# Router logits from the first norm's rows and the attention's output operands, in a one-core decoder layer

## The reference

```
x1 = layernorm(x + retention(x))             # 16 heads of 16, decayed scores, group norm over a sequence
x2 = layernorm(x1 + att(x1, ctx) @ Wo.T + bo)
logits = x2 @ router_w.T                     # 8 experts
p = softmax(logits); the two largest, scaled to sum 1
y  = sum over the two experts of p_e * (gelu(x2 @ w_fc[e] + b_fc[e]) @ w_proj[e] + b_proj[e])
out = layernorm(x2 + y)                      # a layernorm has no weights: (v - mean) * rstd
```

## Time and profile before

| what | us |
|---|---|
| median of 3 runs | 994.58 (993.51 to 995.72) |
| profiled execution | 990.76 |
| its span | 988.7 |
| TensorE busy in the span | 924.2 (93%) |
| TensorE weight loads busy | 822.0 (83%) |
| VectorE busy | 664.0 (67%) |
| ScalarE busy | 605.2 (61%) |
| GpSimd busy | 385.0 (39%) |
| row_max of 128x512 on VectorE (L1267), mean of 128 | 0.682 |

### The profile page before, as it was taken

The page is one execution under the profiler, slowest core; times in us unless marked ns, Lnnn a source line. Parts: engine busy times, 40 slices in busy tenths (PEclk is TensorE's granted clock), DMA queues, the critical chain, the costliest instruction groups (busy, mean ns, idle before and its releaser), DMA issues.

```text
span 988.7 us, 29856 instructions
## 1 busy us (share of the span) xinstructions
PE 924.2 (93%) x10845; PEld 822.0 (83%) x10845; DVE 664.0 (67%) x1977; ACT 605.2 (61%) x1528; POOL 385.0 (39%) x639
## 2 busy tenths in 40 slices
PE   5899999999999999999888999999999999999950
PEld 4788888888888888888667899999999999999950
DVE  3577777777877877877734677575755775665536
ACT  4556656656556666666446567565755765665536
POOL 0324555555544656664523522222222323232223
PEclk9999999999999999999989999999999999999985
DMA  8111141112111111122112453523435343533228
GB/s 279 50 34 56 61 142 45 56 55 66 56 49 45 62 56 61 55 64 85 44 30 44 119 130 58 138 44 53 129 53 139 79 103 53 129 48 46 45 37 336
DMA packets 57362, 79.91 MB, mean 81 GB/s; under 512 B 5728, under 2 KB 46048, under 8 KB 57120
## 3 DMA queue, kind: packets, MB, share of 16 engines
q1 hardware_dynamic: 41504, 58.50, 18.5%
q0 software_dynamic: 13536, 18.16, 10.8%
q10 hardware_dynamic: 2208, 1.73, 0.6%
HBM read 52.10 MB, written 29.71 MB: 83 GB/s over the span
## 4 chain that ended last, share of the span: by engine, by line
PE 79%; ACT 6%; DVE 5%; issue 4%; DMA 2%; SPq 1%; POOL 1%; ACTq 0%; DVEq 0%; POOLq 0%
PE bank L820 16%; PE bank L834 11%; PE bank L511 11%; PE bank L836 5%; PE bank L647 4%; PE bank L673 4%; PE bank L718 3%; PE bank L573 3%; PE bank L626 3%; PE bank L694 3%; PE bank L598 3%; PE bank L593 2%; ACT h_f L1161 2%; PE bank L732 2%; ACT last_out L1237 1%
## 5 line engine op out<-in xcount | busy, mean ns | idle before, releaser
L820 PE MATMUL bank<-xs_hi,w_both 128*128 128x256 f32 x1152 | 241.6, 287 | 0.0
L1155 ACT ACTIVATE h_parts<-bank,bfc_s 128x256 fp32r<-128x256 f32 x288 | 140.0, 486 | 155.3 <-PE bank L820 150.6
L1714 POOL DMA_INDIRECT residual_sum<-y_w,meta_i x72 | 116.9, 1624 | 300.4 <-DVE y_w L1532 267.0
L1490 DVE TENSOR_TENSOR h_parts<-h_f,h_parts 128x256 fp32r<-128x256 f32 x288 | 121.5, 426 | 143.9 <-ACT h_f L1161 138.4
L834 PE MATMUL bank<-w_both,h_parts 128*128 128x512 f32 x544 | 200.0, 398 | 1.1 <-DVE h_parts L1490 1.1
L820 PEld LDWEIGHTS bank<-xs_hi,w_both 128*128 128x128 f32 x1152 | 191.0, 190 | 7.8 <-issue 1.7
L820 PE MATMUL bank<-xs_lo,w_both 128*128 128x256 f32 x576 | 162.7, 282 | 0.0
L836 PE MATMUL bank<-w_both,h_parts 128*128 128x256 f32 x544 | 153.0, 281 | 0.0
L1161 ACT ACTIVATE h_f<-bank,bfc_s 128x256 f32<-128x256 f32 x288 | 139.4, 484 | 3.9 <-DVE h_parts L1490 3.4
L834 PEld LDWEIGHTS bank<-w_both,h_parts 128*128 128x128 f32 x544 | 102.5, 188 | 19.9 <-DVE h_parts L1490 3.5
L820 PEld LDWEIGHTS bank<-xs_lo,w_both 128*128 128x128 f32 x576 | 109.4, 190 | 0.1
(11 more groups left out here) (184 smaller groups left out, 2139.7 us busy)
## 6 DMA issues: line engine op xcount, KB each, us to landing
rows<-sent_rows SPq DMA_DIRECT2D x37, 258.0 KB
xc_raw<-in_turned SPq DMA_DIRECT2D x32, 256.0 KB, 3.0
w_raw<-in_w_fc SPq DMA_DIRECT2D x8, 1024.0 KB
w_raw<-in_w_proj SPq DMA_DIRECT2D x8, 1024.0 KB
x_t<-in_x SPq DMA_DIRECT2D x32, 128.0 KB, 2.2
residual_sum<-x_row SPq DMA_DIRECT2D x32, 128.0 KB, 1.7
last_in<-residual_sum SPq DMA_DIRECT2D x7, 512.0 KB, 7.3
result<-last_out SPq DMA_DIRECT2D x7, 512.0 KB, 2.7
```

Of the source, the lines that this page charges most:

```text
L820: last = mm(ps_h(g, j), w[:, at:at + P], v[:, k, :], start=(n == 0), stop=(n == 3 * NCH - 1))
L1155: A(h_hi[j % 4][:, :], ps_h(g, j), ACT.Gelu_apprx_tanh, bias=bias)
L1490: V.tensor_tensor(h_lo[j % 4][:, :], h_f[j % 2][:, :], h_hi[j % 4][:, :].bitcast(f32), ALU.subtract).then_inc(s["h_split"], 1)
L1714: G.indirect_dma_start(total, bass.IndirectOffsetOnAxis(meta_i[:, half:half + 1], 0), y_w[:, half, :], None, compute_op=ALU.add)\
```

## The change

With P the attention rows before the output projection, the rows ahead of the second norm are v = x1 + bo + P Wo.T, and x2 = (v - mean) * rstd. The logits of x2 are rstd * (v R - mean * colsum(R)), with R the router's weights turned. The change computes v R as x1 R + bo R + P (Wo.T R):

- **Once**, at the end of step 1 (`fold`, `fold_bias`, `fold_out`): the product Wo.T R, 256 x 8, is put beside `wo_s` as columns 256 to 263; bo R and the column sums of R go to `lg_c`. For it a second, turned form of Wo is loaded into a part of `w_raw`, which stands idle then, and SyncE waits for the fold before it loads the first expert's weights there. `got_late` counts one load more.
- **Per sequence**: `qx` also multiplies x1T with `rt_s` into columns 256 to 263 of its bank; ScalarE copies them to one of three `lg_x1` in `qx_out`. `att_proj` has 264 columns where it had 256.
- `lg_out` on VectorE is three linked operations behind `ln2_stats`: mean times column sums plus bo R, plus `lg_x1`, plus the 8 columns of `ps_f`. It leaves out rstd, which `pick` multiplies into the difference of the two largest; their order is the same without it.
- `x2_turn`, `logits` and `x2_T_out` are gone. `rank`, which overwrites the columns in `ps_f`, waits for `lg_out` of the next sequence where it waited for the first operation of `ln2_stats`; `o_turn` waits for `put`.
- In VectorE's even step `put` stands behind `ln2_norm`. The same moves are made in the drain and the slots beside it.

```diff
 wq_s = ab("wq_s", [P, NCH, C])
-wo_s = ab("wo_s", [P, NCH, C])
+wo_s = ab("wo_s", [P, NCH, C + E])
...
 l2rstd = ab("l2rstd", [P, 1])
-x2T = ab("x2T", [P, NCH, T])
+bo_T = ab("bo_T", [P, NCH, T])
+lg_c = ab("lg_c", [P, 2, E])
+lg_mean = ab("lg_mean", [P, 2, E])
+lg_x1 = [ab(f"lg_x1_{i}", [P, E]) for i in range(3)]
...
+wo_turned = w_raw[:, 0:NCH * C].rearrange("p (m n) -> p m n", m=NCH)
+RAW = slice(C, C + E)
+
...
                 .then_inc(s["consts_expert"], 16)
+            sp.wait_ge(s["folded"], 2)
+            apart(sp)
             load_weights(0)
...
         if first(c, 1):
-            pe.wait_ge(s["got_late"], 64)
+            pe.wait_ge(s["got_late"], 80)
         for m in range(NCH):
             for k in range(NCH):
                 last = mm(ps_g[:, m * P:(m + 1) * P], wq_s[:, k, m * P:(m + 1) * P], x1T[:, k, :],
                           start=(k == 0), stop=(k == NCH - 1))
+        for k in range(NCH):
+            last = mm(bank_g[:, RAW], x1T[:, k, :], rt_s[:, k, :], start=(k == 0), stop=(k == NCH - 1))
         last.then_inc(s["qx"], 1)
...
         pe.wait_ge(s["o_out"], c.n + 1)
-        if not first(c, 1):
-            pe.wait_ge(s["lg_out"], c.n)
+        if first(c, 2):
+            pe.wait_ge(s["folded"], 2)
+        else:
+            pe.wait_ge(s["rank_read"], c.n - 1)
         for i in range(HPT):
...
+    def fold():
+        pe.wait_ge(s["got_late"], 80)
+        for k in range(NCH):
+            tr(ps_f[:, k * P:(k + 1) * P], bo_s[:, k * P:(k + 1) * P], ident)
+        for k in range(NCH):
+            at = slice(C + k * E, C + (k + 1) * E)
+            for m in range(NCH):
+                mm(ps_f[:, at], wo_turned[:, m, k * P:(k + 1) * P], rt_s[:, m, :],
+                   start=(m == 0), stop=(m == NCH - 1))
+        for m in range(NCH):
+            last = mm(ps_f[:, C + 2 * E:C + 3 * E], stat_w, rt_s[:, m, :],
+                      start=(m == 0), stop=(m == NCH - 1))
+        last.then_inc(s["fold"], 1)
+
+    def fold_bias():
+        pe.wait_ge(s["folded"], 1)
+        for m in range(NCH):
+            last = mm(ps_f[:, 0:E], bo_T[:, m, :], rt_s[:, m, :], start=(m == 0), stop=(m == NCH - 1))
+        last.then_inc(s["fold"], 1)
+
     def att_proj(c):
         pe.wait_ge(s["att_back_out"], c.n + 1)
         for k in range(NCH):
-            last = mm(ps_f[:, 0:C], attT[:, k, :], wo_s[:, k, :], start=(k == 0), stop=(k == NCH - 1))
+            last = mm(ps_f[:, 0:C + E], attT[:, k, :], wo_s[:, k, :], start=(k == 0), stop=(k == NCH - 1))
         last.then_inc(s["att_proj"], 1)
-    def x2_turn(c):
-        pe.wait_ge(s["x2_done"], c.n + 1)
-        if not first(c, 1):
+    def rank(c):
+        if c.n < B - 1:
+            pe.wait_ge(s["lg_out"], c.n + 2)
+        else:
             pe.wait_ge(s["rank_read"], c.n)
-        for k in range(NCH):
-            last = tr(ps_f[:, k * P:(k + 1) * P], x2_row[c.r][0][:, k * P:(k + 1) * P], ident)
-        last.then_inc(s["x2_T"], 1)
-
-    def logits(c):
-        pe.wait_ge(s["x2_T_out"], c.n + 1)
-        for k in range(NCH):
-            last = mm(ps_f[:, 0:E], x2T[:, k, :], rt_s[:, k, :], start=(k == 0), stop=(k == NCH - 1))
-        last.then_inc(s["logits"], 1)
-
-    def rank(c):
...
             run(y_back, At(k))
-            run(x2_turn, At(k - 3))
             run(att_values, At(k - 2))
-            run(logits, At(k - 3))
             run(prep_v, At(k + 1))
             run(o_turn, At(k - 2))
             run(max_turn, At(k - 1))
@@ -780,13 +800,14 @@
             run(gn_mean, At(k))
             run(y_back, At(k))
             run(max_scores, At(k - 1))
-            run(x2_turn, At(k - 3))
             run(att_values, At(k - 2))
-            run(logits, At(k - 3))
             run(prep_v, At(k + 1))
             if k < B - 1:
                 run(o_turn, At(k - 2))
                 run(max_turn, At(k - 1))
+        if k == 1:
+            fold()
...
             (bo_s[:, :], bo.partition_broadcast(P), "got_late"),
+            (wo_turned, wo_o.rearrange("(m p) n -> p m n", p=P), "got_late"),
             (rt_s[:, :, :], router_t.rearrange("(k p) n -> p k n", p=P), "got_late"))
...
         act.wait_ge(s["qx"], c.n + 1)
+        if not first(c, 3):
+            act.wait_ge(s["lg_out"], c.n - 2)
+            apart(act)
+        A(lg_x1[c.n % 3][:, :], bank_g[:, RAW], ACT.Copy)
...
-    def x2_T_out(c):
-        act.wait_ge(s["x2_T"], c.n + 1)
-        A(x2T[:, :, :].rearrange("p k t -> p (k t)"), ps_f[:, 0:C], ACT.Copy).then_inc(s["x2_T_out"], 1)
+    def fold_out():
+        act.wait_ge(s["fold"], 1)
+        A(bo_T[:, :, :].rearrange("p k t -> p (k t)"), ps_f[:, 0:C], ACT.Copy)
+        for k in range(NCH):
+            A(wo_s[:, k, C:C + E], ps_f[:, C + k * E:C + (k + 1) * E], ACT.Copy)
+        A(lg_c[:, 0, :], ps_f[:, C + 2 * E:C + 3 * E], ACT.Copy, scale=-float(T * C)).then_inc(s["folded"], 1)
+        act.wait_ge(s["fold"], 2)
+        A(lg_c[:, 1, :], ps_f[:, 0:E], ACT.Copy).then_inc(s["folded"], 1)
...
     def lg_out(c):
-        dve.wait_ge(s["logits"], c.n + 1)
-        V.tensor_copy(lg[:, :], ps_f[:, 0:E]).then_inc(s["lg_out"], 1)
+        if first(c, 1):
+            dve.wait_ge(s["folded"], 2)
+        V.scalar_tensor_tensor(out=lg_mean[:, 0, :], in0=lg_c[:, 0, :], scalar=l2mv[:, 0:1], in1=lg_c[:, 1, :],
+                               op0=ALU.mult, op1=ALU.add).then_inc(s["lg_shift"], 1)
+        dve.wait_ge(s["lg_shift"], 2 * c.n + 1)
+        dve.wait_ge(s["qx_out"], c.n + 1)
+        V.tensor_tensor(lg_mean[:, 1, :], lg_x1[c.n % 3][:, :], lg_mean[:, 0, :], ALU.add)                    .then_inc(s["lg_shift"], 1)
+        dve.wait_ge(s["lg_shift"], 2 * c.n + 2)
+        V.tensor_tensor(lg[:, :], ps_f[:, RAW], lg_mean[:, 1, :], ALU.add).then_inc(s["lg_out"], 1)
     def pick(c):
         dve.wait_ge(s["lg_out"], c.n + 1)
@@ -1352,7 +1379,9 @@
         ch.link(V.max(top[:, :], lg[:, :]), apart)
         if not first(c, 1):
             dve.wait_ge(s["share_chain"], SHARE * (c.n - 1) + 1)
-        V.tensor_tensor(gap[:, :], top[:, 1:2], top[:, 0:1], ALU.subtract).then_inc(s["gap_done"], 1)
+        dve.wait_ge(s["ln2_rstd"], c.n + 1)
+        V.scalar_tensor_tensor(out=gap[:, :], in0=top[:, 1:2], scalar=top[:, 0:1], in1=l2rstd[:, 0:1],
+                               op0=ALU.subtract, op1=ALU.mult).then_inc(s["gap_done"], 1)
         ch.link(V.max_index(top_i[:, :], top[:, :], lg[:, :]))
...
             run(ln2_stats, At(k - 3))
+            run(lg_out, At(k - 3))
+            run(ln2_norm, At(k - 3))
             run(put, At(k - 4))
-            run(ln2_norm, At(k - 3))
             run(gn_moments, At(k))
             for r in range(NT):
                 run(att_max, At(k - 1), r)
             run(max_twice, At(k - 1))
             run(gn_centre, At(k))
-            run(lg_out, At(k - 3))
             run(ln1_stats, At(k))
             run(att_norm, At(k - 2))
             run(ln1_sum, At(k))
```

More of the change, by code:

```diff
@@ L61, in link, with decoder_kernel @@
             then(self.eng)
-def decoder_kernel(nc, x, turned, kv_blocks, w_qkv, gn_scale, gn_shift, wq_t, wk_t, wv_t, wo_t, bo,
+def decoder_kernel(nc, x, turned, kv_blocks, w_qkv, gn_scale, gn_shift, wq_t, wk_t, wv_t, wo_t, wo_o, bo,
                    router_t, w_fc, b_fc, w_proj, b_proj, decay_c, small_c, bits_c, out):
@@ L277, in decoder_kernel @@
             rden_done att_norm att_back att_back_out att_proj
-            ln2_chain ln2_var ln2_rstd x2_done x2_again x2_T x2_T_out logits lg_out
+            ln2_chain ln2_var ln2_rstd x2_done x2_again fold bo_turned folded lg_shift lg_out
             top_chain gap_done picked ranked rank_read put_chain placed share_chain shared
@@ L382, in _ @@
             sp.dma_start(bits_f, bits_c).then_inc(s["got_mix"], 16)
-            sp.dma_start(wo_s[:, :, :], wo_t.rearrange("(k p) n -> p k n", p=P)).then_inc(s["got_late"], 16)
+            sp.dma_start(wo_s[:, :, 0:C], wo_t.rearrange("(k p) n -> p k n", p=P)).then_inc(s["got_late"], 16)
             load(At(2))
@@ L789, in step @@
                         run(max_turn, At(k - 1))
+                if k == 1:
+                    fold()
+                    fold_bias()
             def between():
@@ L874, in rank_out @@
                     rank(At(B - 2))
-                if j == 8:
-                    x2_turn(At(B - 1))
-                if j == 10:
-                    logits(At(B - 1))
             def rank_last(j):
@@ L898, in drain @@
                 rank(At(B - 4))
-                x2_turn(At(B - 3))
                 max_scores(At(B - 1))
-                logits(At(B - 3))
                 att_values(At(B - 2))
@@ L920, in drain @@
                 fc0(6)
-                x2_turn(At(B - 2))
                 proj0(5)
                 fc0(7)
-                logits(At(B - 2))
                 pe.wait_ge(s["max_split"], B)
@@ L1098, in step @@
                     run(y_out, At(k))
-                    run(x2_T_out, At(k - 3))
                     run(o_out, At(k - 2))
@@ L1130, in step @@
```

(16 more changed lines are left out.)

## The result

The changed kernel took 1000.52 us (median of 4 runs, 998.82 to 1001.32) against 995.02 for the kernel before (4 runs): ratio on record 1.007, 95% interval 1.0051 to 1.0089 (the two medians alone give 1.0055). Timed again beside more runs it took 1002.63 (6 runs) against 993.10 (17 runs): 1.0101, 1.0077 to 1.0125. So it is slower by 0.5 to 1.3%. The forecast was 1007, the added sum 12.3 us.

A forecast was written before the change was run, and what follows sets the result against it. TensorE bounds the steady stage, with VectorE close behind at four places. Pairs 8.1, load 0.7, fold 3.0, early raw product 0.5 and drain 0 sum to 12.3 us: 1003.1, plus 3.8 carried over, 1007 us; own range 1002 to 1012, overall 992 to 1013.

The forecast's parts named there:

- The pair: Two attention steps in the steady stage: 0.38 + 0.20 = 0.58 us longer, +8.1 us over 14 pairs.
- The raw product: Added TensorE product of x1T with the router weights, four passes behind L617: 0.45 us per sequence (0.45 to 0.54).
- third view: Weight loads set beside VectorE's timeline: four places stand close to VectorE, with 0.03 to 0.22 us of room.
- the gap operation: VectorE operation taking a third input at no extra price; if 0.1 more in even steps, +1.4 us over 14 pairs.
- The drain: Last stage: removed work against the raw product at the lower clock and the lg links; 0, between -2.7 and +2.4 us.
- The start: First steps: load +0.7, fold +3.0 and raw product in steps 0 to 2 +0.5 us.
- The load's 0.7: Turned output weights, 0.26 MB more in the queue that brings the padding at the start: +0.7 us (0 to 0.7).
- the fold's own 3.0: Fold at the end of step 1 delays step 2's scores by 3.1 us, some tenths absorbed: +3.0 us (1.5 to 4).
- rival 4: New idle time costs TensorE its clock, falling once behind the fold: 5 us, giving 1012 us; chance 0.04.
- Rival 1: TensorE alone is the bound and the new waits don't come: 992 us, or 987; chance 0.20.
- Rival 2: Half of the new waits is absorbed, rooms at L664 and L711 being larger than read: 1002 us; chance 0.12.
- Rival 3: The three lg links and the wait before rank reach the path in even steps: +7 us, 1014; chance 0.07.

The follow-up runs named there:

- delay: The kernel before with one spare 128x256 VectorE addition ahead of the row_max copy in odd steps; 998.80 us in a single run.
- raw_late: The changed kernel with the raw product, and ScalarE's copy of it, moved from qx to ahead of the max transpose; 993.64 us, 1.0013 to the kernel before.
- no_raw: The changed kernel without the raw product from the second sequence on; routing differs, so only pairs compare: 29.994 us a pair.
- pick_late: best0 with VectorE's choice of experts moved behind the retention masks (ret_p) in half of the steps; 999.02 us, 1.0061 to the kernel before.
- best0: The changed kernel with the edits of raw_late and fold_mid together; 993.14 us, 1.0004 to the kernel before.
- before_again: The kernel before, unchanged, run once more; 993.15 us.
- fold_mid: The changed kernel with the fold spread in step 2 and the turned weights loaded separately behind the padding; 999.53 us, 1.0055 to the kernel before.

## Why the prediction was right, and where its sizes were off

- **The mechanism stands.** The sum said that TensorE's shorter work would turn into a wait for the row_max copy, with the raw product paid in full behind it. The wait is there, 0.64 us on the weight load where 0.54 was forecast, each pair. TensorE's busy share is 97.6 (97 forecast). delay shows that the room was 0.08 us, raw_late that place and not length decides, no_raw that the removals without the raw product are worth 0.05 us a pair.
- **The pair: +0.58 forecast, +0.34 measured.** The raw product was mis-sized: 0.35 us, not 0.45, twice a pair, 0.20 in all. I took the time of four passes of 128 columns for four of 8. The remaining 0.04 is a balance of errors that nearly cancel:
  - At the attention scores the kernel before waited 0.25 us for ret_p (block 1.97), and the later scores of the changed kernel don't (1.72): a fifth place near VectorE that my third view missed, since no idle time names it. This took 0.25 off.
  - From the even scores to L711 a pair gained 0.22 (10.64 to 10.42) where 0.31 was forecast. The 0.09 is the lg copy, whose removal I counted in full. It had stood in the pause between the linked y_c and x_pre: from start to start they take 0.62 us with it and 0.61 without.

```profile
203.26 0.48 DVE L1290 SCALAR_TENSOR_TENSOR y_c<-bank,gm,gnw 128x256 f32<-128x256 f32 x1
203.66 0.16 DVE L1346 COPY lg<-bank 128x8 f32<-128x8 f32 x1
203.88 0.48 DVE L1298 SCALAR_TENSOR_TENSOR x_pre<-y_c,grstd,xb 128x256 f32<-128x256 f32 x1
```

```profile
181.68 0.48 DVE L1310 SCALAR_TENSOR_TENSOR y_c<-bank,gm,gnw 128x256 f32<-128x256 f32 x1
182.29 0.48 DVE L1318 SCALAR_TENSOR_TENSOR x_pre<-y_c,grstd,xb 128x256 f32<-128x256 f32 x1
```

  - The way from the odd L711's load to the scores' grew by 0.49 (205.71 to 209.47 before, 183.91 to 188.16 after); 0.38 of it is added work (0.35 + 0.03), 0.03 was forecast for L617, and 0.08 was not. There `pick` takes 0.14 longer ahead of x1 (MAX8 to x: 1.09 us, 0.95 before), as the prediction had feared of the gap operation with 0.1, and L617, now L625, waits for x1.
  - The last 0.04 lies between the odd scores and the next even ones; I didn't trace it.
- **The drain and what follows: 0 forecast, -1.4 measured** (with the end of the fourteenth pair in it), within what two runs of one kernel differ by (1.8 to 2.7 us). The bounds held; the value can't be judged.
- **The start: +4.2 forecast, +7.3 measured** (+5.6 to +7.3 over the four executions). The load's 0.7 is about right (0.8 at the padding's end). So is the fold's own 3.0 (2.91 and 2.75 on the chain, about 0.3 absorbed). The sum put the clock at nothing: rival 4, given 0.04 and 5 us, happened in part. Behind the fold the slower clock cost 1.5 and 1.7 us, and the first execution lost another 1.5 ahead of it, where the other fall stands (2.4 less the load's 0.8). That the fold at the end of step 1 brings the later fall is shown by five executions against eight; what in it does so is open. The 0.5 for the raw product in the first steps was not measured by itself. The step-2 scores started at 46.75, not near 45.
- **Rival 1** (TensorE alone is the bound) fell to the waits and to delay. Here the Trainium skill's rule (Perfetto Trace Analysis, Identifying the Most-Contended Engine) to optimize the engine of highest occupancy pointed the wrong way: TensorE at 150.00 of 150.00 gained next to nothing from less work (0.05 us a pair in no_raw), and by its weight loads it led as well (129.25 against VectorE's 116.34). Its warning that matmul busy time misleads held. **Rival 2** said +4 in the stage and 1002 us, which is about what came, and nearer to it than the forecast's +8.1 and 1007, but for another reason: it held that the rooms were larger than I read, and the rooms came out as read (0.08 us at L664 by delay, 0.22 at L711), with the wait at L674 longer than forecast, not shorter. **Rival 3** (links before rank) did not come: the rank product's loads wait 0.8 us for lg in ten pairs, four times in all. pick_late shows the place where it does come.
- **The total.** 12.3 us was forecast on a span of 988.7, 10.3 came. The 3.8 us carried over to the median of the runs should not have been: the kernel before repeated at 993.1 over 17 runs, and the changed kernel's profile lay at its own median. Two errors of more than 3 us, start (+3.1) and pairs (-3.3 over the same 14), had opposite signs; that the sum of 12.3 came within 2 us of the 10.3 is luck to that extent.

## What to carry over

When an engine reads as fully busy, set its waiting instructions beside the ends of their inputs: where that room is 0.1 us, two engines are the bound in turn, and an edit is worth only what the next wait behind it lets through. Put added work where the engine waits anyway, and expect the next wait close behind: here four kernels with different work on TensorE (before, raw_late, no_raw, best0) all took 29.98 to 30.04 us a pair. Twice here a small operation stood in the pause between two linked ones and was free there: removing it gained nothing (lg), and moving it cost time (row_max copy). One-off work at the start has to be priced with its place: here the same fold was followed by the slower clock at the end of step 1 and not in step 2.

## What I had not expected of the hardware

- Four fp32 passes of 8 columns with 128x128 weights took 0.35 us, 0.088 each, against 0.111 each for 128 columns (0.89 for eight): sixteen times fewer columns saved a fifth.
- A wait can hide in a row with no idle time: the scores block took 1.72, 1.97 and 2.07 us for the same instructions, 1.69 or 1.70 us from the end of ret_p each time.
- A VectorE copy of 16 columns was free between two linked operations (0.57 us from start to start with it and without) and cost 0.23 us a pair elsewhere.
- The idle share alone does not tell when the clock falls. In the changed kernel 2 us with TensorE busy 1.32 were followed by 0.50 to 0.57, in both executions. In before_again 0.33 of 2 us (40 to 42 us) and in fold_mid 2.22 of 4 us were not followed by a fall.
